# Vision tower: the last unit of each chunk's half projects its three query and key blocks ahead of the values

## What is computed

```
q, k, v = split_heads(xn @ Wq), split_heads(xn @ Wk), split_heads(xn @ Wv)   # xn = layernorm(h)
scores  = q @ k.T / 8          # per image and head; layer 0 with a causal mask
h       = h + concat(softmax(scores) @ v) @ Wo
```

## Time and profile before

| | |
|---|---|
| median of 3 runs | 957.4 us |
| profiled execution | 958.55 us, of which 956.8 us are its span |
| TensorE busy with matmuls | 922.3 us, 96% of the span |
| VectorE, ScalarE busy | 575.1 us, 546.1 us |
| attention of layer 0, first to last scores | 44.18 to 221.27 us |
| attention of layer 1, first to last scores | 317.28 to 493.73 us |

### The profile page before, as it was taken

The page is one execution under the profiler, slowest core; times in us unless marked ns, Lnnn a source line. Parts: engine busy times, 40 slices in busy tenths (PEclk is TensorE's granted clock), DMA queues, the critical chain, the costliest instruction groups (busy, mean ns, idle before and its releaser), DMA issues.

```text
span 956.8 us, 18575 instructions
## 1 busy us (share of the span) xinstructions
PE 922.3 (96%) x7105; PEld 857.4 (90%) x7105; DVE 575.1 (60%) x1251; ACT 546.1 (57%) x1571; POOL 155.6 (16%) x173
## 2 busy tenths in 40 slices
PE   5999999999898999999999999999999999999997
PEld 5878888888877878888889999999999999999997
DVE  4666574758999574765656778544364534554333
ACT  4665464637675754655654745665566646565442
POOL 0232121311000221221210000620111101111012
PEclk9999999999999999999999999999999999999999
DMA  9310000001100210000002011202020111100001
GB/s 332 132 47 1 1 2 1 2 2 45 45 1 1 88 45 1 2 1 1 2 1 89 1 46 48 85 1 89 2 88 1 46 45 45 45 1 1 1 14 39
DMA packets 8796, 34.46 MB, mean 36 GB/s; under 512 B 642, under 2 KB 5122, under 8 KB 5380
## 3 DMA queue, kind: packets, MB, share of 16 engines
q1 hardware_dynamic: 8708, 33.28, 9.7%
HBM read 32.06 MB, written 1.22 MB: 35 GB/s over the span
## 4 chain that ended last, share of the span: by engine, by line
PE 47%; issue 33%; DVE 9%; POOL 6%; ACT 3%; DMA 1%; POOLq 0%; SPq 0%; DVEq 0%; ACTq 0%
PE D L579 17%; PE O L579 11%; POOL h L363 4%; PE T L766 4%; PE O L780 4%; PE S L755 3%; PE S L579 3%; PE D L601 2%; PE S L749 1%; PE O L695 1%; POOL h L375 1%; DVE probsT L1341 1%; PE T L637 1%; PE T L624 1%; DMA raw<-in_x 1%
## 5 line engine op out<-in xcount | busy, mean ns | idle before, releaser
L1584 DVE TENSOR_TENSOR hid<-work,hid 128x300 fp32r<-128x300 f32 (+1 forms) x256 | 135.2, 555 | 179.4 <-ACT hid L1133 179.3
L579 PE MATMUL O<-hid,wslot 128*128 128x300 f32 (+3 forms) x1680 | 239.9, 301 | 0.0
L579 PEld LDWEIGHTS O<-hid,wslot 128*128 128x128 f32 x1680 | 232.4, 188 | 0.6
L579 PE MATMUL D<-xn,wslot 128*128 128x300 f32 (+3 forms) x1368 | 220.9, 307 | 0.0
L579 PEld LDWEIGHTS D<-xn,wslot 128*128 128x128 f32 x1368 | 197.5, 189 | 3.7
L1129 ACT ACTIVATE work<-D,prm 128x300 f32<-128x300 f32 (+1 forms) x128 | 66.4, 519 | 167.8 <-PE D L579 167.5
L1024 ACT ACTIVATE probs<-S,negmax 111x111 f32<-111x111 f32 (+1 forms) x352 | 117.5, 359 | 53.8 <-DVE negmax L1326 53.6
L558 POOL TENSOR_TENSOR probs<-probs,rsum 111x444 f32<-111x444 f32 (+1 forms) x88 | 80.9, 920 | 368.9 <-DVE rsum L1334 368.9
L579 PE MATMUL S<-xn,wslot 128*128 128x300 f32 (+3 forms) x864 | 134.1, 302 | 0.0
L579 PEld LDWEIGHTS S<-xn,wslot 128*128 128x128 f32 x864 | 123.4, 189 | 0.1
L363 POOL TENSOR_TENSOR h<-h,work 128x300 f32<-128x300 f32 (+1 forms) x56 | 49.3, 900 | 284.3 <-DVE work L1603 284.3
(11 more groups left out here) (179 smaller groups left out, 1160.6 us busy)
## 6 DMA issues: line engine op xcount, KB each, us to landing
raw<-in_moe SPq DMA_DIRECT2D x16, 1024.0 KB, 4.8
raw<-in_attn SPq DMA_DIRECT2D x7, 1024.0 KB, 4.8
work<-in_x SPq DMA_DIRECT2D x2, 1008.0 KB, 8.4
w2f<-in_attn SPq DMA_DIRECT2D x1, 1024.0 KB, 12.5
raw<-in_ffn SPq DMA_DIRECT2D x1, 1024.0 KB, 4.8
w2f<-in_ffn SPq DMA_DIRECT2D x1, 1024.0 KB, 5.1
raw<-in_x SPq DMA_DIRECT2D x2, 504.0 KB, 6.0
out<-h SPq DMA_DIRECT2D x3, 300.0 KB, 2.8
```

The source lines that it names most:

```text
L579: mm = pe.matmul(psum, a, b, start=(first and k == 0), stop=(k == 3 * n - 1))
L1584: nc.vector.tensor_tensor(moe_hid(s, 1), moe_g(s)[:, 0:w], moe_hid(s, 0).bitcast(F32), ALU.subtract).then_inc(m_hid, 1)
```

## The change

A new function `blocks_first(u)` says how many of a unit's query and key blocks stand ahead of the values. It gives 0 in the units with an output projection, all blocks of the unit when the unit is the last of its half, and 1 otherwise. TensorE and ScalarE both use it; VectorE's order is unchanged.

```diff
+        def blocks_first(u):
+
+            p, n = place_in_half(u) if u < NUNIT else (0, 0)
+            if out_due(u) is not None:
+                return 0
+            return len(qk_blocks(u)) if p == n - 1 else 1
@@ TensorE
-                        for i in blocks[:1]:
+                        for i in blocks[:blocks_first(u)]:
                             project_qk(i)
                     if 0 <= u - 1 < NUNIT:
                         values(u - 1)
@@ TensorE
-                    for i in blocks[0 if due is not None else 1:]:
+                    for i in blocks[blocks_first(u):]:
                         project_qk(i)
@@ ScalarE
-                    n = 0 if due is not None else 1
+                    n = blocks_first(u)
                     for i in blocks[:n]:
                         move_q(i)
```

## The result

The changed kernel takes 966.13 us (median of 4 runs, 964.97 to 966.89) against 957.75 us for the kernel before beside it: a ratio of 1.0086 with a 95% interval of 1.0072 to 1.0099, 8.4 us slower. The profiled execution is the fastest of the four, 964.97 us, and 6.4 us above the profiled one of the kernel before (958.55).

What follows compares the result with a forecast made beforehand. TensorE, at 96% of the span, was taken to bound the kernel, with VectorE's chain delaying it in attention. The places' terms 6.0 + 1.35 + 1.1 + 1.4 - 1.1 = +8.8 us on 957.4 gave 966.2 us, range 961.0 to 969.5.

Steps and rivals of the forecast that it cites:

- a chain of 2.88 us: Each unit, through VectorE: `row_max`, exponentials, `invert_sums`, `move_t`, then values on TensorE; forecast as 2.89 us from `row_max` to values.
- The unit without `apply`: Unit 5, both layers: no `apply` is due behind `low_out`, so the change gains, -1.1 us for both.
- the units with a stall already there: Unit 2 of layer 1 and unit 17 of both layers: whole shift of `low_out` goes through, +1.35 and +1.4 us.
- unit 14: Both layers: `low_out` 1.67 us later, half of the lateness falls into idle time; 0.55 us each, +1.1 us.
- step 1: TensorE, units 8 to 9: values start 2.06 us later behind two blocks; the 0.54 us wait ahead of the scores goes.
- a cousin: Unit 3 of layer 1: clock could halve behind 2.7 us of idle time, giving 969.4 us; 12% together with dearer lateness.
- At its full level in every slice: Premise from the profile page of the kernel before: TensorE's clock is at its full level throughout the 956.8 us span.
- The wait goes and nothing takes its place: Rival: all twelve waits of the scores for ScalarE vanish, 6.2 us faster, 951.2 us; 8%.
- step 4: TensorE, unit 9: values can't start before 125.22 against 124.07, so the place costs 1.15 us, the 0.54 gain included.
- The two cancel: Rival: VectorE's lateness costs half at the ten places with `apply`, about 961 us, or a tenth, no change (6%).
- The lateness costs more: Rival: the whole shift of 1.35 to 1.67 us goes through everywhere, 969 to 970 us; 12% with the clock case.
- The signs to watch: Profile after: L749 waits about 2.1 us, ten more units wait for `probsT`, VectorE waits for `high_out` at twelve places.

Runs made afterwards that it cites:

- Experiment 2: Kernel before with only ScalarE's new order in the twelve places, TensorE's order kept: 970.77 us, ratio 1.0150.
- experiment 5: Changed kernel with `low_out` of the twelve units moved into the next unit, between the second `row_max` and `invert_sums`: 950.63 us, ratio 0.9927.
- experiment 4: Changed kernel plus nine unread 128x128 matmuls in TensorE's idle stretch of layer 1, unit 3: 964.55 us, ratio 1.0079.
- experiment 3: Changed kernel with `low_out` behind `apply` and `add_halves` in the twelve units: 956.26 us against 958.03 us, ratio 0.9983.
- experiment 7: Changed kernel with only two weight quarters of layer 1 moved from unit 2 to unit 3: 965.43 us, ratio 1.0080.
- 6: Changed kernel with `low_out` in the next unit and two weight quarters of layer 1 made in unit 3 instead of 2: 949.28 us, ratio 0.9912.

## Why the prediction was right, point by point

**The mechanism held.** The forecast was +8.8 us, measured are +8.4. `low_out` is held at the head of VectorE's stream (1.06 us of idle time before it), `row_max` follows, and TensorE pays behind a chain of 2.88 us. Experiment 2 makes a loss of the same kind, and a larger one, without touching TensorE, experiment 5 takes the hold away and turns the loss into a gain of 7.1 us with the change's own order on TensorE and ScalarE. The unit without `apply` gained, the units with a stall already there had no slack, unit 14 lost about half: the ranking of the places is as forecast. The other terms of the sum held: the values take 0.91 us to the scores (117.45 - 116.54), `high_out` starts 1.02 us behind them, `low_out` 0.58 us behind that.

**Two terms were off, and they offset each other.** The first is step 1, "the values move behind two blocks, each 1.03 us, so they start 2.06 us later". From the first block to the values it is 116.54 - 113.58 = 2.96 us, where the step makes it 1.10 + 2.06 = 3.16. The step took the start-to-start times of the old order for the new one, 1.10, 1.03 and 1.03 us; in the new order they are 1.01, 0.93 and 1.02. So TensorE saves 0.81 us and not 0.54, `low_out` is 0.2 us less late, and each place is 0.1 to 0.2 us cheaper, unit 5 0.3 to 0.4 us better. With the clock held up the twelve places sum to 3.07 + 4.71 - 1.44 = 6.3 us, not 8.8; experiment 4, which holds it up at the one place, is 6.5 us slower than the kernel before beside it (964.55 against 958.03).

The second is the clock, which stood under the rivals ("a cousin") at a price of up to 3.2 us and outside the sum. It fell at the place that was named, unit 3 of layer 1, at a cost of 1.44 us; the idle stretch was 2.77 us, forecast 2.7. The text gave it as unlikely; in the profiled execution it happened. The two quicker executions of the changed kernel, the profiled one among them, have a mean granted clock of 0.998, the two slower ones 0.996; the kernel before has 0.998 to 1.000. So the slower two probably had more or longer falls, and falls are the likely reason why the median lies 2 us above the 6.3 of the chain. Only one execution was traced, so this is argued.

The way, the places and the mechanism are therefore no luck, but the closeness is: a sum that was 2.5 us too high met a clock that the sum left out, and 8.8 against 8.4 hides both.

One premise on the clock was read too strongly. "At its full level in every slice" rests on digits of 9, and such a digit means 0.9 or more of a slice of 24 us. The changed kernel's row has the same forty nines with the fall in it, and in the kernel before the window from 954 to 956 us, where TensorE has no work left, is at 0.54 under a 9. Falls of this size show only in windows of a few us.

**The rivals.** "The wait goes and nothing takes its place" fails by the hold on VectorE alone: with that gone the saving is real and even larger than its 6.2 us. The number by which it was to be decided was wrong, though: by step 4 the cost is the shift less 0.20, with the 0.54 us already inside, so a place begins to lose at a shift of 0.20 us and not of 0.75. The runs agree with step 4: in unit 9 of layer 0 `row_max` is 1.16 us later in the changed kernel and the place costs 0.95; in experiment 3 it is 0.14 us later and the place gains 0.07. What fails is the reading of the view of waits as a budget. The advice of the Trainium skill ("Perfetto Trace Analysis", Optimization Strategies), to work on those that block the matmul engine, names the right engine only if the one that would block next is looked up too. "The two cancel" fell: `apply` and `add_halves` did not close up behind the wait (118.14 to 121.30 is 3.16 us, 117.83 to 120.98 was 3.15). "The lateness costs more" fell in its first part, since where there was slack the place costs the shift less the slack; its clock part held at one place.

**The signs to watch.** The waits of L749 fell to 2.1 us as said, and VectorE waits for `high_out` at all twelve places. TensorE waits for `probsT` behind ten places, but only seven of these waits are new; at unit 17 and at unit 2 of layer 1 they were there and grew (in unit 18 from 0.43 to 1.57 us). From the first block of unit 8 to the values of unit 9 it is 10.60 us and was 9.65: +0.95 where 1.15 was said. `row_max` of unit 9 starts 3.85 us behind its scores. From the scores of unit 5 to those of unit 6 it is 0.91 and 0.82 us less, where 0.54 was said.

## What to carry to other kernels

When a producer is moved later to fill a wait on one engine, follow its result through every stream that consumes it: a consumer whose turn comes before its data holds all that is queued behind it, however independent that is. Move the consumer by as much as the producer, into a gap where its engine waits anyway; here that one line turns 8.4 us of loss into 7.1 us of gain. And read how much lateness an engine can still absorb (from the start of its chain to where the bound engine needs the end) before reading how long the bound engine waits.

## What the runs showed of the hardware beyond that

Whether TensorE's granted clock falls from its full level to half (2.4 to 1.2 GHz) behind an idle stretch is not set by the length of that stretch alone. In experiment 2, unit 3 of layer 1, it stayed at 1.00 behind 2.47 us, as the window below shows. It fell behind 2.77 us (the changed kernel) and behind 1.74 us (experiment 3). Stretches of 1.57 to 1.59 us stand at ten places in attention of the changed kernel, experiment 4 and experiment 7, and it fell behind one of them (experiment 7, unit 18 of layer 0). The stretch of 1.80 to 1.82 us between the layers stands in all nine traces, and it fell behind that of experiment 7 alone.

```profile
349.58 0.61 PE L773 MATMUL T<-ident,probs 111*111 111x111 f32 x4 [2.47 <-DVE probsT L1348]
```

```profile
350.00:352.00 2.00, 1.96 (x24) 1.62 (x23) 1.47 (x4) 2.00 (x12) 0.93 (x1) 1.00 0.96 401
```

A fall in the traced executions cost from 0.5 us (behind 1.80 us, experiment 7) to 3.2 us (unit 17, experiment 7); the one in the changed kernel cost 1.4. Versions with short idle stretches repeat best: in those of experiments 5 and 6 TensorE's longest waits for `probsT` are 1.2 and 0.6 us, and their runs lie within 0.6 and 0.2 us of each other. With longest waits of 1.6 to 2.5 us the runs lie within 4.2 us (experiment 3), 4.8 us (7), 6.7 us (4) and 7.5 us (2). The time goes with the clock there: in each of these four the slowest execution has the lowest mean granted clock of its version (0.995, 0.995, 0.993 and 0.990), where the quickest has 0.999 or 1.000. That the scatter is the clock's is thereby likely; where the falls lie is known for one execution of each version only, and what decides a single fall stays open.
